# Gated linear attention with routed memories: the order of small and full-width products in the scan loop

## Chip, core and metric

One core of one Trainium2 chip. The metric is the device time of the whole program in microseconds, on that core. The engines are TensorE (PE: matmuls and transposes; its weight loads are PEld), VectorE (DVE), ScalarE (ACT), GpSimd (POOL, which issues the indirect DMAs) and SyncE (SP, which issues most of the others).

## What is computed

```python
x = x + attn(layernorm(x))      # x is (8, 512, 256)
x = x + moe(layernorm(x))       # 8 experts, top-k per expert

# attn: every token goes to 2 of 4 memories (at most 256 tokens each) and to a shared one
q, k, v = tx @ w_q, tx @ w_k[m], tx @ w_v[m]          # 4 heads, 32 and 64 wide
gk = log_sigmoid(tx @ w_gk1[m] @ w_gk2[m] + b_gk[m]) / 16
def step(S, (q, k, v, g)):      # over the tokens of a sequence
    S = S * exp(g)[..., None] + k[..., None] * v[..., None, :]
    return S, einsum('k,kv->v', q, S)
o = routed outputs, weighted and put back + shared output
o = o * rsqrt(mean(o * o) + eps) * norm_w * silu(x @ w_g)
return o @ w_o
```

All of it is float32.

## The kernel before

It has four parts. First the layer norm, the transposes of x and the gate product (0 to 60 us). Then the scan stage, 24 steps, which the change touches. Then the router's search for the tokens of each expert, and at last the experts. Every engine has its program written out by hand; engines meet at semaphores, and an engine that waits holds up everything behind it in its own program.

The scan stage treats a group of 512 tokens at a time: groups 0 to 6 and 23 are the shared memory's batches; groups 7 to 22 (`routed(g)`) are each two memories of one batch, half a group each. A group is cut into 8 chunks of 64 tokens. In the chunk, `scores` multiplies decayed keys `kd` and decayed queries `qd` (32 x 32 tiles of TensorE, 64 products, each two records in the trace); `masked` (L1028) copies them to `am` under the causal mask; `updates` (tiles of 64 x 32) multiplies keys and values of each chunk; `states` (L1047, L1049, L1053) chains the chunks on VectorE and writes `tst`; and `outputs` adds `qd` times `tst` and `am` times values. All four kinds are small products. The projections are full width: `gate` (512 or twice 256 columns), `keys`, `queries`, and `values` in two halves of 256 tokens. `keys_t` (L1577) and `rows_t` (L1570) are transposes. Nearly every product is issued by the helper at L1522, so the trace tells them apart by their tiles.

Decay factors come by a longer way. `gate` for group s+1 fills a bank, VectorE adds the bias (`gate_in`, L1016 or L1019), ScalarE makes a softplus of it in three steps (`softplus`, L692 to L696), VectorE finishes (`gate_log`, L1035), scans (`scan`, L1062) and takes distances (`distances`, L1071 to L1075), and ScalarE exponentiates (`decays`, L722 to L731). VectorE then multiplies keys and queries by them (`decayed_keys`, L1082; `decayed_queries`, L1089). ScalarE also empties banks: `values` (L685), `keys_in` (L714), `rows_in` (L679), and `group_out` (L704, L706), which takes the outputs of the group before and counts `d_ob`; TensorE waits for `d_ob` after `queries`.

In a step, TensorE's order is: values(s, 0), gate(s+1), outputs(s-1), keys(s), queries(s), the extra work, keys_t(s), values(s, 1), rows_t(s+2, 0), scores(s), rows_t(s+2, 1), updates(s). The extra work belongs to finished batches (`step_of(s, first)`: one batch every second step from `first` on): combine and head squares from step 11 (odd), `turned` and `gated` from 12 (even), `project` and `residual` from 13 (odd), `row_stats` from 14 (even), `norm_t` from 15 (odd), `route` and `router` from 16 (even). These products use the banks that `scores` writes, so `scores` waits for their readers.

GpSimd moves rows by indirect DMA, eight per slot: `scatter_slot` (L400) brings a batch's rows to its memories in steps 3 to 11, `gather_slot` (L407) brings outputs back in steps 10, 12 and so on to 22, and once behind the loop. SyncE loads the routed groups, stores the outputs (`store_group` waits for `d_ob`) and moves x. The choice of memories (`top`, `room`, `assign`, `counts`) runs in steps 0 to 2.

## Time and profile before

| what | value |
|---|---|
| median of 3 runs | 857.61 us (856.16 to 858.35) |
| profiled execution | 861.46 us, span 859.5 us |
| busy: TensorE, VectorE, ScalarE, GpSimd | 726.9, 392.4, 309.1, 237.3 us |
| chain that ended last | TensorE 80%, VectorE 10%, issue 5%, ScalarE 3% |
| scan stage, 60 to 489 us | TensorE idle about 29 us |

The span is the time from the first to the last instruction of the profiled execution. "Granted clock" is TensorE's clock as a share of 2.4 GHz; it is either 1.00 or 0.50, so a value between them says how long each level held. "issue" behind a gap says that the engine waited for nothing that the profile shows.

### The profile page before, as it was taken

Reading aid. Unit: us, or ns where it says so; the run is one execution under the profiler, and the core shown is the slowest. Engines: PE = TensorE matmul, PEld = TensorE weight load, DVE = VectorE, ACT = ScalarE, POOL = GpSimd, SP = SyncE. Lnnn points to the kernel's source line nnn. Section 1 sums busy time; section 2 is a strip of 40 time slices with the busy share of each in tenths; the row PEclk is TensorE's granted clock in tenths of the full one; section 3 lists DMA queues with packets and bytes.
Section 4 is the critical chain, followed back from the end, with each engine's and each line's share of the span. In section 5 each row is a group of like instructions: output and inputs, shape, how many; then the busy total and the mean of one; then the engine's idle time right before and its main releaser. Section 6 shows DMA issues by size and latency. Waiting matters only on the chain.

```text
span 859.5 us, 22577 instructions
## 1 busy us (share of the span) xinstructions
PE 726.9 (85%) x9727; PEld 552.5 (64%) x9727; DVE 392.4 (46%) x1132; ACT 309.1 (36%) x629; POOL 237.3 (28%) x232
## 2 busy tenths in 40 slices
PE   3998899989999999999999777202499999999994
PEld 3875665677777788888887556202347667766683
DVE  7517854544466666776576635698001001100111
ACT  2654433544354455565464324100141231123100
POOL 5300053554545031221213120000624342211222
PEclk9999988998899999999999966555599999999998
DMA  7940133333345244434254313700452454231212
GB/s 241 399 127 2 52 112 104 111 136 106 129 136 165 91 153 145 150 118 155 91 156 128 113 37 118 231 0 0 131 192 46 133 141 122 29 100 19 26 20 29
DMA packets 75435, 96.58 MB, mean 112 GB/s; under 512 B 11322, under 2 KB 67042, under 8 KB 74187
## 3 DMA queue, kind: packets, MB, share of 16 engines
q1 hardware_dynamic: 62506, 69.78, 24.8%
q0 software_dynamic: 12288, 25.12, 11.9%
q8 instruction: 76, 1.25, 0.6%
q10 hardware_dynamic: 544, 0.27, 0.1%
q14 instruction: 21, 0.16, 0.1%
HBM read 53.78 MB, written 41.55 MB: 111 GB/s over the span
## 4 chain that ended last, share of the span: by engine, by line
PE 80%; DVE 10%; issue 5%; ACT 3%; another core or an unknown queue 1%; DMA 1%; POOL 0%; DVEq 0%; POOLq 0%; ACTq 0%
PE bank L1522 49%; PE attn L1522 20%; PE bank L1480 3%; PE bank L1570 2%; DVE arena L1338 2%; PE bank L1577 1%; PE attn L1469 1%; PE attn L1835 1%; DVE gs L1402 1%; DVE gs L1397 1%; PE attn L1662 1%; DMA arena<-in_L_attn_x_dram 1%; PE attn L1686 1%; DVE st L909 0%
## 5 line engine op out<-in xcount | busy, mean ns | idle before, releaser
L1522 PE MATMUL bank<-xT,arena 128*128 128x256 f32 (+1 forms) x480 | 135.1, 429 | 0.7 <-ACT lg L641 0.7
L1522 PE MATMUL bank<-arena,xT 128*128 128x256 f32 (+1 forms) x448 | 133.2, 445 | 1.5 <-issue 1.5
L407 POOL DMA_INDIRECT big<-o_m,gidx x64 | 67.7, 1057 | 186.9 <-PE bank L1522 136.3
L1522 PE MATMUL attn<-arena 32*32 32x32 f32 (+3 forms) x5824 | 96.8, 221 | 22.0 <-issue 17.3
L1522 PEld LDWEIGHTS attn<-arena 32*32 32x32 f32 (+2 forms) x5824 | 79.8, 118 | 47.7 <-issue 37.6
L1522 PEld LDWEIGHTS bank<-xT,arena 128*128 128x128 f32 x480 | 90.2, 192 | 28.9 <-issue 17.4
L1522 PEld LDWEIGHTS bank<-arena,xT 128*128 128x128 f32 x448 | 88.8, 207 | 29.7 <-issue 17.8
L1449 DVE TENSOR_TENSOR arena<-bank,b2b 128x256 f32<-128x256 f32 x32 | 13.6, 425 | 203.3 <-PE bank L1522 203.3
L400 POOL DMA_INDIRECT x_c<-big,sidx x64 | 69.6, 1087 | 132.2 <-PE bank L1522 93.7
L479 POOL DMA_INDIRECT out_dram<-arena,idxs x32 | 49.7, 1553 | 131.2 <-DVE arena L1456 100.5
L466 POOL DMA_INDIRECT arena<-x_p,idxs x32 | 32.3, 1009 | 137.3 <-DVE idxs L1411 101.0
L1028 DVE COPY_PREDICATED arena<-causal,attn 128x1024 f32<-128x1024 int32 x24 | 31.6, 1316 | 79.1 <-PE attn L1522 79.1
L894 ACT ACTIVATE big<-attn,b1c 128x512 f32<-128x512 f32 x32 | 22.0, 687 | 116.7 <-PE attn L1522 116.7
L685 ACT ACTIVATE arena<-bank 128x512 f32<-128x512 f32 x48 | 28.7, 598 | 89.9 <-PE bank L1522 81.9
L1522 PE MATMUL bank<-xT,big 128*128 128x256 f32 x256 | 55.9, 379 | 0.0
L1522 PE MATMUL bank<-gs,big 128*128 128x256 f32 x256 | 55.7, 379 | 0.0
L1522 PEld LDWEIGHTS bank<-xT,big 128*128 128x128 f32 x256 | 48.6, 190 | 8.3 <-issue 1.9
L1522 PEld LDWEIGHTS bank<-gs,big 128*128 128x128 f32 x256 | 48.6, 190 | 7.9 <-issue 1.4
L886 ACT ACTIVATE arena<-attn 128x512 f32<-128x512 f32 x16 | 8.7, 594 | 73.9 <-PE attn L1835 71.8
L894 ACT ACTIVATE big<-bank,b1c 128x512 f32<-128x512 f32 x32 | 22.0, 688 | 32.9 <-PE bank L1522 32.9
L1049 DVE SCALAR_TENSOR_TENSOR arena<-arena,bank 128x64 f32<-128x64 f32 x112 | 31.5, 282 | 4.0
L1522 PE MATMUL attn<-arena,xT 128*128 128x512 f32 x64 | 30.6, 624 | 2.8 <-ACT arena L886 2.8
(240 smaller groups left out, 1063.7 us busy)
## 6 DMA issues: line engine op xcount, KB each, us to landing
x_c<-zeros SPq DMA_DIRECT2D x8, 1024.0 KB, 12.9
xT<-x_c SPq DMA_DIRECT2D x16, 512.0 KB
o_m<-arena SPq DMA_DIRECT2D x16, 512.0 KB
xT<-in_L_ffn_W_dram SPq DMA_DIRECT2D x8, 1024.0 KB, 8.6
gs<-in_L_ffn_W_dram SPq DMA_DIRECT2D x8, 1024.0 KB, 9.2
arena<-in_L_attn_x_dram SPq DMA_DIRECT2D x8, 512.0 KB, 7.7
xT<-in_L_attn_x_dram SPq DMA_DIRECT2D x8, 512.0 KB
out_dram<-xT SPq DMA_DIRECT2D x8, 512.0 KB, 5.3
```

The costliest lines, as they stand in the source:

```text
L400: nc.gpsimd.indirect_dma_start(x_c[b], bass.IndirectOffsetOnAxis(sidx[:, k, t:t + 1], 0), xn[:, t, :], None, bounds_check=MROWS - 1, oob_i ...
L407: nc.gpsimd.indirect_dma_start(og[:, b % 2, k, j, :], None, o_m[b], bass.IndirectOffsetOnAxis(gidx[:, k, t:t + 1], 0), bounds_check=MROWS ...
L466: nc.gpsimd.indirect_dma_start(xe[:, e % 3, j, :], None, x_p, bass.IndirectOffsetOnAxis(idxs[:, e, j:j + 1], 0), bounds_check=B * S - 1, o ...
L479: nc.gpsimd.indirect_dma_start(outf, bass.IndirectOffsetOnAxis(idxs[:, e, j:j + 1], 0), ye[:, e % 2, j, :], None, bounds_check=B * S - 1, ...
L685: nc.scalar.activation(vv[:, g % 2, 2 * h:2 * h + 2, :], bank[7].rearrange("p (j d) -> p j d", j=2), ACT.Copy).then_inc(d_vs, 1)
L894: nc.scalar.activation(ht[:, r, f, :], bank[2 + f % 4][:, :], ACT.Gelu_apprx_tanh, bias=b1c[:, col(f)]).then_inc(e_gl, 1)
L1028: nc.vector.copy_predicated(am[:, :, :, :], causal[:, :].bitcast(I32).unsqueeze(1).unsqueeze(1).to_broadcast([P, NH, TB, CH]), attn[:, :, ...
L1049: chained(nc.vector.scalar_tensor_tensor(vst[:, c, :], vst[:, c - 1, :], fe[:, g % 2, c - 1:c], u, ALU.mult, ALU.add))
L1338: ins = nc.vector.tensor_scalar(cmp[:, c, :], pt[:, :], cand[:, c:c + 1].bitcast(F32), None, ALU.is_ge, ALU.add, accum_out=reached[:, c:c ...
L1480: ins = nc.tensor.matmul(bank[4 + j][:, 0:D + M], xT[:, b, k, P * j:P * j + P], wgg[:, k, :], start=(k == 0), stop=(k == 1))
L1522: return nc.tensor.matmul(out_, l, r, start=a, stop=z, skip_group_check=True)
L1570: ins = nc.tensor.transpose(bank[4][:, P * j:P * j + P], xin[:, n % 2, j, P * k:P * k + P], ident[:, :])
```

## The change

TensorE's order becomes updates(s-1), gate(s+1), outputs(s-1), keys(s), queries(s), extra work, keys_t(s), scores(s, 0), values(s, 1), rows_t(s+2, 0), scores(s, 1), values(s+1, 0), rows_t(s+2, 1). The scores come in two parts of two token blocks (256 tokens) each, and `d_s` counts both. In `outputs` the product of `am` and values comes first and that with the states last. VectorE writes `kd` and `qd` (`qd` in two halves) ahead of the next scan, and `residual` follows the scan. In step 0 and 1 `top` is moved, in step 2 both `assign` stand behind the distances. The indirect DMAs wait for other events: behind `outputs`, behind each part of the scores, and behind `updates`. No arithmetic is added or removed, but for `qd`'s second instruction.

```diff
             def scatter_slot(b, s):
                 if b >= 2:
                     pool.wait_ge(scat[b % 2], 16 * 2 * TB * (b // 2))
-                pool.wait_ge(d_u, s)
+                pool.wait_ge(d_o, s)
                 scatter(b, 0, 3)
-                pool.wait_ge(d_o, s)
-                scatter(b, 3, 6)
-                pool.wait_ge(d_q, s + 1)
-                scatter(b, 6, 8)
+                pool.wait_ge(d_s, 2 * s + 1)
+                scatter(b, 3, 5)
+                pool.wait_ge(d_s, 2 * s + 2)
+                scatter(b, 5, 7)
+                pool.wait_ge(d_u, s + 1)
+                scatter(b, 7, 8)
 
             def gather_slot(b, s):
                 last = FIRST + 2 * b + 1
@@ -429,11 +431,11 @@
                 if b >= 2:
                     pool.wait_ge(f_oa, b - 1)
                 if b < LAST:
-                    pool.wait_ge(d_u, s)
-                    gather_back(b, 0, 3)
                     pool.wait_ge(d_o, s)
-                    gather_back(b, 3, 6)
-                    pool.wait_ge(d_q, s + 1)
+                    gather_back(b, 0, 4)
+                    pool.wait_ge(d_s, 2 * s + 1)
+                    gather_back(b, 4, 6)
+                    pool.wait_ge(d_s, 2 * s + 2)
                     gather_back(b, 6, 8)
...
@@ -825,9 +827,9 @@
 
             softplus(0)
             decays(0)
+            values(0, 0)
             for s in range(NG):
                 head, turn, route, stats = (step_of(s, f) for f in (11, 12, 15, 14))
-                values(s, 0)
                 if s + 1 < NG:
                     softplus(s + 1)
                 if 1 <= s <= NG:
@@ -849,6 +851,8 @@
                     decays(s + 1)
                 if routed(s + 2):
                     rows_in(s + 2, 1)
+                if s + 1 < NG:
+                    values(s + 1, 0)
...
             def decayed_queries(g):
@@ -1086,8 +1090,10 @@
                 dve.wait_ge(d_q, g + 1)
                 if g >= 1:
                     dve.wait_ge(d_o, g)
-                nc.vector.scalar_tensor_tensor(qd[:, :], bank[6], float(HDK) ** -0.5, eq[:, :],
-                                               ALU.mult, ALU.mult).then_inc(d_qd, 1)
+                for part in range(2):
+                    t = slice(CAP * part, CAP * part + CAP)
+                    nc.vector.scalar_tensor_tensor(qd[:, t], bank[6][:, t], float(HDK) ** -0.5, eq[:, t],
+                                                   ALU.mult, ALU.mult).then_inc(d_qd, 1)
...
             for s in range(NG):
                 head, turn, out_, stats, shift_, logit = (step_of(s, f) for f in (11, 12, 13, 14, 15, 16))
-                if s == 0:
-                    decayed_keys(0)
-                    decayed_queries(0)
                 if s >= 2:
                     states(s - 1)
+                if s == 1:
+                    states(0)
+                    top(0)
+                    decayed_keys(1)
                 if s + 1 < NG:
                     gate_in(s + 1)
-                if s == 0:
-                    top(0)
-                    masked(0)
-                    states(0)
-                if s == 1:
-                    decayed_keys(1)
-                    decayed_queries(1)
...
-                if s == 2:
-                    assign(0)
...
                 if shift_ is not None:
@@ -1249,29 +1246,33 @@
                     combine(head)
                 if turn is not None:
                     gated(turn)
+                if s + 1 < NG and s >= 2:
+                    gate_log(s + 1)
+                if s != 1:
+                    decayed_keys(s)
+                decayed_queries(s)
+                if s < 2:
+                    gate_log(s + 1)
                 if s + 1 < NG:
-                    gate_log(s + 1)
                     scan(s + 1)
-                if s >= 2:
-                    decayed_keys(s)
+                if out_ is not None:
+                    residual(out_)
                 if s + 1 < NG:
                     distances(s + 1)
-                if s >= 2:
-                    decayed_queries(s)
+                if s == 1:
+                    top(1)
+                if s == 2:
+                    assign(0)
+                    assign(1)
+                if logit is not None:
+                    router(logit)
+                if head is not None:
+                    head_squares(head)
+                if stats is not None:
+                    row_stats(stats)
+                masked(s)
                 if s == 1:
                     room()
-                if s == 2:
-                    assign(1)
-                if head is not None:
-                    head_squares(head)
-                if out_ is not None:
-                    residual(out_)
-                if logit is not None:
-                    router(logit)
-                if stats is not None:
-                    row_stats(stats)
-                if s >= 1:
-                    masked(s)
...
-            def scores(g):
-                pe.wait_ge(d_qd, g + 1)
-                if g >= 1:
...
-                for j, h, c, lo in product(range(TB), range(NH), range(2), range(2)):
+            def scores(g, part):
+                pe.wait_ge(d_qd, 2 * g + part + 1)
+                if part == 0:
+                    if g >= 1:
+                        pe.wait_ge(d_ob, g)
+                    turn, out_, route, logit = (step_of(g, f) for f in (12, 13, 15, 16))
+                    if turn is not None:
+                        pe.wait_ge(f_ont, 2 * turn + 2)
+                    if out_ is not None:
+                        pe.wait_ge(f_x1, 2 * out_ + 2)
+                    if route is not None:
+                        pe.wait_ge(f_xt2, 2 * route + 2)
+                    if logit is not None:
+                        pe.wait_ge(f_l8, logit + 1)
+                for j, h, c, lo in product((2 * part, 2 * part + 1), range(NH), range(2), range(2)):
...
             def outputs(g):
+                pe.wait_ge(d_am, g + 1)
+                for j in range(TB):
+                    for i in range(2):
+                        for c, h in ((0, i), (1, 3 - i), (1, 1 - i), (0, 2 + i)):
+                            s = slice(CH * c, CH * c + CH)
+                            mm(bank[h][half(c, h), HDV * j:HDV * j + HDV], am[s, h, j, :],
+                               vv[s, g % 2, j, HDV * h:HDV * h + HDV], j == 0, True)
                 pe.wait_ge(d_t, g + 1)
-                pe.wait_ge(d_am, g + 1)
                 heads = [lo // CH for _, lo, _ in pieces(g)]
-                opened = set()
                 for j in range(TB):
                     for c in range(2):
                         n = 2 * j + c
...
-                            mm(bank[h][half(c, h), HDV * j:HDV * j + HDV], qd[r, t], tst[r, n, :],
-                               (c, h) not in opened, False)
-                            opened.add((c, h))
-                for j in range(TB):
-                    for i in range(2):
-                        for c, h in ((0, i), (1, 3 - i), (1, 1 - i), (0, 2 + i)):
-                            s = slice(CH * c, CH * c + CH)
-                            ins = mm(bank[h][half(c, h), HDV * j:HDV * j + HDV], am[s, h, j, :],
-                                     vv[s, g % 2, j, HDV * h:HDV * h + HDV], False, True)
+                            ins = mm(bank[h][half(c, h), HDV * j:HDV * j + HDV], qd[r, t], tst[r, n, :], False, True)
                 ins.then_inc(d_o, 1)
...
             gate(0)
+            values(0, 0)
             for s in range(NG):
-                values(s, 0)
+                if s >= 1:
+                    updates(s - 1)
                 if s + 1 < NG:
                     gate(s + 1)
                 if s >= 1:
                     outputs(s - 1)
-                if s < NG:
-                    keys(s)
-                    queries(s)
+                keys(s)
+                queries(s)
                 if s >= 1:
                     pe.wait_ge(d_ob, min(s, NG))
                 if step_of(s, 12) is not None:
@@ -1754,17 +1754,19 @@
                     norm_t(step_of(s, 15))
                 if step_of(s, 16) is not None:
                     route(step_of(s, 16))
-                if s < NG:
-                    keys_t(s)
-                    values(s, 1)
-                    if s == 1:
-                        counts()
-                    if routed(s + 2):
-                        rows_t(s + 2, 0)
-                    scores(s)
-                    if routed(s + 2):
-                        rows_t(s + 2, 1)
-                    updates(s)
+                keys_t(s)
+                scores(s, 0)
+                values(s, 1)
+                if routed(s + 2):
+                    rows_t(s + 2, 0)
+                scores(s, 1)
+                if s + 1 < NG:
+                    values(s + 1, 0)
+                if s == 1:
+                    counts()
+                if routed(s + 2):
+                    rows_t(s + 2, 1)
+            updates(NG - 1)
             outputs(NG - 1)
             turned(LAST - 1, (4, 7))
             project(LAST - 1, 5)
```

## Rows read from the trace of the kernel before

**Rows 1.** The page: DMA queues, and the costliest groups (busy, mean ns, idle before).
```profile
q8 instruction: 76, 1.25, 0.6%
...
L400 POOL DMA_INDIRECT x_c<-big,sidx x64 | 69.6, 1087 | 132.2 <-PE bank L1522 93.7
```

**Rows 2.** Windows by stage: length, busy of each engine, granted clock, DMA share, GB/s.
```profile
104.00:148.40 44.40, 39.64 (x807) 26.58 (x797) 21.00 (x46) 15.05 (x31) 20.40 (x19) 0.85 0.32 105
...
196.00:235.00 39.00, 37.27 (x737) 30.39 (x730) 19.04 (x40) 16.00 (x31) 18.80 (x18) 0.87 0.36 122
...
284.00:289.00 5.00, 4.50 (x22) 3.62 (x23) 2.21 (x7) 0.53 (x1) 0.00 (x0) 0.66 0.35 104
```

**Rows 3.** Timeline of TensorE, step 4: start, duration, line, count, idle before.
```profile
139.16 0.33 PE L1522 MATMUL attn<-arena 32*32 32x32 f32 x5 [0.39 <-issue]
...
142.01 1.16 PE L1522 MATMUL bank<-arena 64*32 64x64 f32 x55 [0.96 <-issue]
143.10 3.78 PE L1522 MATMUL bank<-arena,xT 128*128 128x256 f32 x8
```

**Rows 4.** Timeline of TensorE, steps 13 and 14.
```profile
301.60 1.46 PE L1522 MATMUL attn<-arena 32*32 32x64 f32 x128
...
304.26 1.99 PE L1522 MATMUL bank<-arena,xT 128*128 128x256 f32 x8
306.09 1.89 PE L1522 MATMUL bank<-xT,arena 128*128 128x256 f32 x8
```

**Rows 5.** Waits of TensorE, 59.8 to 490 us (last row: 110 to 530): total, times, longest.
```profile
PE attn L1522 <- issue: 15.6, 33, 1.1
PE bank L1522 <- issue: 6.7, 7, 1.9
PE bank L1577 <- ACT arena L706: 1.9, 1, 1.9
...
PE attn L1522 <- DVE arena L1053: 4.0, 2, 2.9
```

**Rows 6.** Groups by form, TensorE, 59.8 to 490 us: busy, mean ns, idle before.
```profile
L1522 PE MATMUL attn<-arena 32*32 32x64 f32 x1536 | 40.6, 225 | 4.0 <-issue 3.7
L1522 PE MATMUL attn<-arena 32*32 32x32 f32 x1536 | 39.0, 200 | 7.4 <-issue 7.4
...
L1522 PE MATMUL bank<-arena 64*32 64x64 f32 x1191 | 20.5, 235 | 5.8 <-issue 5.2 <-ACT arena L685 0.6
```

**Rows 7.** Windows of 4 us; busy is PE, PEld, DVE, ACT, POOL.
```profile
104.00:108.00 4.00, 2.14 (x125) 1.79 (x115) 2.10 (x6) 1.18 (x4) 0.00 (x0) 0.93 0.01 4
...
192.00:196.00 4.00, 2.80 (x150) 2.01 (x152) 0.60 (x1) 1.97 (x7) 1.19 (x2) 1.00 0.21 73
...
300.00:304.00 4.00, 4.00 (x183) 3.37 (x185) 1.04 (x2) 2.79 (x8) 0.00 (x0) 1.00 0.02 4
```

**Rows 8.** Timeline of all engines, steps 4 and 5.
```profile
143.21 0.23 DVE L1047 COPY arena<-bank 128x64 f32<-128x64 f32 x1 [0.97 <-PE bank L1522]
...
145.37 0.63 DVE L1053 TENSOR_TENSOR arena<-arena 128x448 f32<-128x448 f32 x1
...
149.33 1.94 PE L1522 MATMUL attn<-arena 32*64 32x64 f32 x120
...
152.69 1.21 ACT L706 ACTIVATE arena<-attn 64x512 f32<-64x512 f32 x2
...
154.90 0.63 PE L1577 MATMUL bank<-ident,arena 128*128 128x128 f32 x4
```

**Rows 9.** Timeline of all engines, step 17.
```profile
370.38 1.27 DVE L1132 TENSOR_TENSOR xT<-attn,xT 128x512 f32<-128x512 f32 x2
...
371.37 1.08 ACT L769 ACTIVATE big<-attn 128x512 f32<-128x512 f32 x2 [2.28 <-PE attn L1686]
...
372.04 1.89 PE L1522 MATMUL bank<-arena,xT 128*128 128x256 f32 x8
...
373.77 0.60 PE L1570 MATMUL bank<-ident,xT 128*128 128x128 f32 x4
```

More of the change, by code:

```diff
@@ L728, in decays @@
                 if g >= 1:
-                    act.wait_ge(d_qd, g)
+                    act.wait_ge(d_qd, 2 * g)
                 for half_, at in ((lo, dec), (hi, cum)):
@@ L1024, in masked @@
             def masked(g):
-                dve.wait_ge(d_s, g + 1)
+                dve.wait_ge(d_s, 2 * g + 2)
                 if g >= 1:
@@ L1080, in decayed_keys @@
                 if g >= 1:
-                    dve.wait_ge(d_s, g)
+                    dve.wait_ge(d_s, 2 * g)
                 nc.vector.tensor_tensor(kd[:, :], bank[5], ek[:, :], ALU.mult).then_inc(d_kd, 1)
@@ L1226, in _ @@
                 head, turn, out_, stats, shift_, logit = (step_of(s, f) for f in (11, 12, 13, 14, 15, 16))
-                if s == 0:
-                    decayed_keys(0)
-                    decayed_queries(0)
                 if s >= 2:
                     states(s - 1)
+                if s == 1:
+                    states(0)
+                    top(0)
+                    decayed_keys(1)
                 if s + 1 < NG:
                     gate_in(s + 1)
-                if s == 0:
-                    top(0)
-                    masked(0)
-                    states(0)
-                if s == 1:
-                    decayed_keys(1)
-                    decayed_queries(1)
-                    top(1)
-                if s == 2:
-                    assign(0)
                 if s == FIRST:
@@ L1578, in keys_t @@
                 ins.then_inc(d_kp, 1)
-            def scores(g):
-                pe.wait_ge(d_qd, g + 1)
-                if g >= 1:
-                    pe.wait_ge(d_ob, g)
-                turn, out_, route, logit = (step_of(g, f) for f in (12, 13, 15, 16))
-                if turn is not None:
-                    pe.wait_ge(f_ont, 2 * turn + 2)
-                if out_ is not None:
-                    pe.wait_ge(f_x1, 2 * out_ + 2)
-                if route is not None:
-                    pe.wait_ge(f_xt2, 2 * route + 2)
-                if logit is not None:
-                    pe.wait_ge(f_l8, logit + 1)
-                for j, h, c, lo in product(range(TB), range(NH), range(2), range(2)):
+            def scores(g, part):
[13 more added lines that the diff above has]
+                for j, h, c, lo in product((2 * part, 2 * part + 1), range(NH), range(2), range(2)):
                     lo = lo * CH // 2
@@ L1603, in updates @@
                 pe.wait_ge(d_kt, g + 1)
-                pe.wait_ge(d_qd, g + 1)
+                pe.wait_ge(d_qd, 2 * g + 2)
                 pe.wait_ge(d_vs, 2 * g + 2)
```

## Prediction

> **What bounds the kernel now.** I read the page first. TensorE is by far the busiest engine and carries four fifths of the chain that ended last (the table above), so a change pays where TensorE idles or runs at its lower clock. The windows show where [rows 2]. The scan stage, 24 groups from 60 to 489 us, has two losses. The first is the granted clock: it is 0.85 in 104 to 148.4, 0.87 in 196 to 235 and 0.66 in 284 to 289; the stretch 417 to 422 reads the same as the last. A share of (1 - clock) of each stretch is lost: 0.15 x 44.4 = 6.7, 0.13 x 39 = 5.1, and 0.34 x 5 = 1.7 twice, 15.2 us in all. That is 30.4 us spent at 1.2 instead of 2.4 GHz. The price is seen on one row: the eight records of one `values` half take 3.78 us at the low level and 1.99 at the high one [rows 3, 4].
>
> The second loss is idle time of TensorE: 15.6 + 6.7 = 22.3 us in 40 gaps stand behind "issue", and only 5 us behind another engine [rows 5]. By form [rows 6] the gaps sit before small products: 3.7 + 7.4 = 11.1 us inside `scores`, 5.2 in `updates`, the other 6 in `outputs` and the start of `values`. The order explains the place. `scores` (128 records) and `updates` (48 or 56) stand together, with at most 4 transposes between, and in step 4 they show gaps, 0.39 us in the first and 0.96 in the second; right behind them the clock is at its low level [rows 3]. In step 13 the same sequence runs without a gap and the clock stays up [rows 4]. Windows of 4 us show both kinds of gap [rows 7]: with GpSimd issuing, TensorE is busy 2.80 of 4; without GpSimd and with DMA at 0.01 it is once busy only 2.14 of 4, where scores and updates follow each other; in a third it is busy all 4 with 183 products. So I take two causes: GpSimd's indirect DMAs against small products, and bursts of instructions longer than TensorE's supply.
>
> The program of TensorE comes in 76 packets, 1.25 MB, 16.4 KB each [rows 1]. The Trainium skill (Runtime: NRT & Kernel Launch, Instruction fetch mechanics) says an engine refills in 16 KiB blocks of 256 instructions and that crossing a block is mostly hidden. The packet size agrees; by the "hidden" part gaps would not follow bursts, and moving them would give nothing back (a rival below).
>
> **The change, part by part.** TensorE's work is the same; its order differs. Old step: values half 0, gate, outputs, keys, queries, extras, keys_t, values half 1, scores, updates. New: updates of the group before, gate, outputs, keys, queries, extras, keys_t, half the scores, values half 1, other half, next values half 0. No two kinds of small product touch any more: the longest run is 120 records, where it was 184.
>
> *Clock.* Low stretches follow a run of scores and updates with gaps. With 1.9 us of projection on both sides of every small burst I expect two of nine such stretches to stay (a stretch lasts 3.4 us by 30.4 / 9, 1.7 us lost each): 7 x 1.7 = -11.9. Bounds 0 and -15.2.
>
> *Gaps.* GpSimd issues eight indirect DMAs a slot, about 1.09 us each and a short pause [rows 1]. Before, three start at the end of `updates` and reach into `outputs`, and the last two run into `scores`. Now 3 or 4 start behind `outputs`, over keys and queries (3.7 us), two behind each half of the scores, over a values half (1.9 us). Of the 22.3 us I leave 5.0 in scores (half of each burst is still there), 1.0 in updates and 1.5 in outputs: -14.8. Bounds 0 and -20.8 (1.5 left).
>
> *More switches between small tiles and full ones.* A values half takes 1.83 us start to start behind updates (304.26 to 306.09) and 1.73 behind a transpose at full width (372.04 to 373.77) [rows 4, 9]: 0.10 for the way back. There is one more return per step: 23 x 0.10 = +2.3. Bounds 0, if the last small product is merely longer, and twice that, if the way there costs as much. The Trainium skill (TensorEngine Tiling (Array Packing), Key Properties) states that a change of tiling mode drains TensorE, which speaks against the change; the trace agrees with a small price, and the sum goes by the row.
>
> *New waits, plain steps.* Count from the end of updates(s-1). VectorE needs 2.8 us for `states` (143.21 to 146.00) [rows 8]. Old: that lay under values and gate, 3.7 us. New: gate is done at 1.85, the first half of `outputs` (scores times values, first now) at 2.8; the second half waits for the states to about 2.9. So 0.1 is lost in ungrouped steps, none in routed ones (six updates, 2.4 us). `gate_in` is behind the states, 1.05 us later than the gate's end. From gate end to the end of `group_out` it was 149.33 to 153.90, 4.57 us, and keys_t began at 154.90, behind the queries [rows 8]: slack 1.0, now used up. About +0.2 in five steps, +1.0. Keys_t finds `kd` ready: keys end 1.85 us before queries and the product of 0.67 now goes before the scan. The split costs VectorE about 0.15 us a step (a 256-column operation is about 0.42), behind its own waits for scores.
>
> *New waits, steps with extra work.* The first half of the scores now comes 1.73 + 0.53 = 2.27 us earlier, and that was the cover of everything `scores` waits for. In step 17 keys_t ends at 372.04; the two copies of `norm_t` end at 372.45, `residual` at 371.65 [rows 9]. So +0.4 in the five steps with `norm_t`, +0.4 in step 13 (project's last half plus a residual half of 0.64 less keys_t), +0.3 in steps 12 and 14 (copy of the turned tile 0.75, less 0.43): +3.2. From step 16 on the router's add (0.19) ends inside keys_t.
>
> *First steps.* Step 1: `gate_in(2)` is behind states, top and keys, so group_out and the 1.9 us wait on it [rows 5] grow by 0.9. Step 2: gate(3) waits for `room`, behind masked and counts: +0.5. Both `assign` (20 operations, 4.5 us) now stand ahead of masked(2), which holds back states(2) by 1.3. Sum +2.7. Step 23 has no gate: the wait for states was 4.0 - 2.9 = 1.1 [rows 5], now about 1.5: +0.4. SyncE's queue: the load of a routed group waits for all eight scatters, which now end about 1.3 us into the next step, and it is used a step later; the store of a group stands behind it but waits for `d_ob` 8 us into the step anyhow. The last two gathers end 0.4 us into the next step and `combine` starts 4 us in; a landing of 2 us fits, with 1.5 to spare.
>
> *Behind the loop.* TensorE waits 2.9 us for states(23) [rows 5]; half of `outputs`, 1.0 us, now runs there: -1.0.
>
> Sum: -11.9 - 14.8 + 2.3 + (1.0 + 3.2 + 2.7) + 0.4 - 1.0 = -18.1 us. It is made against the profiled execution (861.46; span 859.5), which lies 3.85 above the median of the runs, 857.61; I take the same difference there: **839.5**. The chip tells 0.3% (2.6 us) from no change.
>
> **Rivals.**
> 1. *More comes back.* All low stretches go and 1.5 us of gaps stay: -15.2 - 20.8 + 8.6 = -27.4, 830; with the new waits at half, 827. For it: step 13 shows the old sequence gapless. Against: gaps appear also without GpSimd.
> 2. *Half comes back.* Gaps move into the halves and four or five low stretches remain: -7.6 - 7.4 + 8.6 = -6.4, 851. For it: the old gaps of 0.4 us come after 39 to 46 small products, and a half has 64.
> 3. *It changes nothing that can be told.* A third comes back, 12 us at most, less 8.6, and up to 2.3 more for the switches: 855 to 860.
> 4. *Slower, nothing comes back.* Gaps and clock belong to the number of small instructions and to GpSimd: +8.6, 866. Against it: the gaps differ by step and place with the same count of instructions. The section of the Trainium skill on instruction fetch, named above, speaks for it, since hidden fetches would leave the length of a burst without effect.
> 5. *Slower, first half of scores late.* It loses its cover of 2.27 us. If whatever it waits for (the residual, `ont`, `d_ob`) arrives just in time for the old place, the loss is 2.27 x 12 = 27 us in place of 3.2, so 863. It decides from 1.5 us in each of the twelve steps with extra work. Against it: in step 17 the last of these is 0.4 us late, not 2.27 [rows 9].
>
> **How the numbers follow.** Forecast (833 to 848) 0.47, rival 1 0.14, rival 2 0.17, rival 3 0.09, rival 4 0.07, rival 5 0.06. Faster is 0.47 + 0.14 + 0.17 = 0.78, same 0.09, slower 0.13. The range leaves out the slower cases and the lowest end of rival 1: 826 to 858.
>
> **What would show it.** The granted clock in 104 to 240 us near 1.00 (clock step), else rival 2 or 4. TensorE's waits: "issue" near 7 to 8 us in place of 22.3, with few behind `updates`; GpSimd's DMAs under full-width products. New waits behind VectorE's states or ScalarE's copies before the first scores half, near 0.4 us each: if they are above 1.5, rival 5. The scan stage, 429 us long, should last about 412. The search and the experts behind it should not change. I would be wrong most easily in how many gaps remain, for no row shows split scores.

## The result and the profile after

The changed kernel takes 869.75 us (median of 4 runs, 867.53 to 871.63), the kernel before beside it 857.98 (856.16 to 861.04): the ratio is 1.0138, 95% interval 1.0105 to 1.0171. It is slower by 1.4%, where 839.5 was forecast. Its profiled execution took 871.63 us, its span is 869.9; the span of before was 859.5. Of all runs below one, at 864.08 us, lay over 1.5% above the fastest of its kernel, and that kernel's ratio ("before, paced 2") leaves it out.

The page of the changed kernel, the rows that answer to [rows 1], with TensorE's share of the span:

```profile
PE 738.2 (85%) x9727; PEld 553.0 (64%) x9727; DVE 394.9 (45%) x1156; ACT 306.4 (35%) x629; POOL 235.0 (27%) x232
...
q8 instruction: 76, 1.25, 0.6%
...
L407 POOL DMA_INDIRECT big<-o_m,gidx x64 | 70.5, 1101 | 185.9 <-PE attn L1523 148.5
...
L400 POOL DMA_INDIRECT x_c<-big,sidx x64 | 64.5, 1008 | 146.2 <-PE attn L1523 123.7
```

The work is the same. What grew is the scan stage. I measure it as "the loop" below, from the start of `keys_t` in step 0 to its start in step 23, read from TensorE's timeline: 69.0 to 485.1 before, 69.5 to 496.7 after, 416.1 us against 427.2. Ahead of it 0.4 us were lost, behind it 1.2 gained. The windows, to set beside [rows 2]:

```profile
104.00:148.40 44.40, 39.48 (x879) 24.88 (x877) 26.55 (x69) 16.31 (x33) 16.02 (x16) 1.00 0.32 105
...
196.00:235.00 39.00, 36.15 (x802) 29.30 (x804) 18.88 (x42) 16.30 (x32) 17.80 (x19) 1.00 0.39 132
284.00:289.00 5.00, 4.50 (x30) 3.53 (x30) 1.30 (x1) 0.19 (x1) 2.31 (x3) 0.66 0.22 69
```

The granted clock is 1.00 where it was 0.85 and 0.87, as forecast. Over the whole loop it is less good: six stretches of 3.4 us at 1.2 GHz, 20.5 us, where nine made 30.7. TensorE's waits from 59.8 to 500 us, to set beside [rows 5]:

```profile
PE attn L1523 <- issue: 12.5, 34, 0.5
PE bank L1523 <- issue: 6.3, 15, 0.6
PE bank L1578 <- ACT arena L708: 3.6, 1, 3.6
PE attn L1523 <- DVE arena L1057: 2.9, 2, 1.5
PE attn L1523 <- ACT big L771: 2.0, 5, 0.4
```

"issue" is 18.8 us in 49 gaps and not 7 to 8. The longest is 0.6 us; before it was 1.9. So the gaps changed in kind: of those behind "issue" from 59 to 500 us the kernel before has eight over 0.8 us, 10.7 us in all, and this one none; the shorter ones rose from 14.8 us to 18.8. A gather step shows where the short ones are. TensorE from 358 us:

```profile
358.63 0.82 PE L1523 MATMUL attn<-arena 32*32 32x64 f32 x64 [0.28 <-issue]
359.37 1.99 PE L1523 MATMUL bank<-arena,xT 128*128 128x256 f32 x8
361.20 0.60 PE L1571 MATMUL bank<-ident,xT 128*128 128x128 f32 x4
361.73 0.79 PE L1523 MATMUL attn<-arena 32*32 32x64 f32 x41
362.98 0.47 PE L1523 MATMUL attn<-arena 32*32 32x64 f32 x23 [0.46 <-issue]
363.38 1.99 PE L1523 MATMUL bank<-arena,xT 128*128 128x256 f32 x8
365.21 0.60 PE L1571 MATMUL bank<-ident,xT 128*128 128x128 f32 x4
365.74 0.84 PE L1523 MATMUL bank<-arena 64*32 64x64 f32 x44
367.02 0.32 PE L1523 MATMUL bank<-arena 64*32 64x64 f32 x4 [0.44 <-issue]
```

and GpSimd's timeline in the same stretch:

```profile
357.08 1.01 POOL L407 DMA_INDIRECT big<-o_m,gidx  x1 [0.30 <-issue]
360.23 1.00 POOL L407 DMA_INDIRECT big<-o_m,gidx  x1 [2.14 <-PE attn L1523]
361.54 1.00 POOL L407 DMA_INDIRECT big<-o_m,gidx  x1 [0.30 <-issue]
364.23 1.00 POOL L407 DMA_INDIRECT big<-o_m,gidx  x1 [1.70 <-PE attn L1523]
365.54 1.00 POOL L407 DMA_INDIRECT big<-o_m,gidx  x1 [0.30 <-issue]
```

Read the two together. The full-width products at 363.38 (eight records) run at their usual speed with a DMA beside them. (Counts of small products here and below are counts of records, two to a product.) A burst of small products runs for about 41 records and stops until 0.4 to 0.5 us behind the end of GpSimd's record: 362.54 and 362.98, 366.54 and 367.02. The pair of DMAs released by one half of the scores starts 0.9 us later, its first lies under the values half, and its second under the next small burst. In steps 3 to 22 it is so in all steps with DMAs but those where the products between ran at 1.2 GHz and gave it time (steps 10, 12, 18 and 22). A stalled burst costs more than its recorded gap: scores part 1 took 363.38 - 361.73 = 1.65 us with a gap of 0.46, where the same burst without a DMA takes 0.77 (382.98 to 383.75, step 17). The lost 0.88 us are nearly twice the gap. In all, this kernel's scores and updates run 31 us over their clean lengths at the full clock. 13 of its updates are stalled under a DMA (1.1 to 1.9 us in place of 0.76, 9.8 us lost); in the kernel before, none was. The Trainium skill (Perfetto Trace Analysis, Tensor Engine Instruction) says that the end of a TensorE record is estimated from the instruction's size, so a gap between records need not be all of a stall; the trace agrees.

By groups of steps the loop changed in three ways (scatter steps 3 to 9; then even steps 10 to 22, which gather, and odd ones 11 to 21):

| us | first 3 | 7 scatter | 7 gather | 6 odd | loop |
|---|---|---|---|---|---|
| before | 49.3 | 124.2 | 134.7 | 107.9 | 416.1 |
| changed | 50.3 | 119.7 | 152.6 | 104.6 | 427.2 |
| before, no indirect DMAs | 49.2 | 107.3 | 130.2 | 100.6 | 387.2 |
| changed, no indirect DMAs | 50.3 | 105.2 | 132.5 | 102.4 | 390.4 |

### The profile page after: what moved, and what is told of

Its sections match the earlier page's. It is cut to its first block, busy times and chain, and to the rows that moved or that the text cites. A ratio compares the mean times of both kernels' runs of the same rounds, so it can differ in the third digit from the quotient of the medians.

```text
span 869.9 us, 22576 instructions
## 1 busy us (share of the span) xinstructions
PE 738.2 (85%) x9727; PEld 553.0 (64%) x9727; DVE 394.9 (45%) x1156; ACT 306.4 (35%) x629; POOL 235.0 (27%) x232
## 3 DMA queue, kind: packets, MB, share of 16 engines
q0 software_dynamic: 12288, 25.12, 11.9%
## 4 chain that ended last, share of the span: by engine, by line
PE 79%; DVE 10%; issue 6%; ACT 3%; DMA 1%; POOL 0%; another core or an unknown queue 0%; DVEq 0%; POOLq 0%; ACTq 0%
PE bank L1523 49%; PE attn L1523 21%; PE bank L1481 4%; DVE arena L1339 2%; PE bank L1571 2%; PE attn L1837 1%; PE attn L1470 1%; DVE gs L1398 1%; ACT big L771 1%; DVE gs L1403 1%; PE bank L1578 1%; PE attn L1661 1%; DMA arena<-in_L_attn_x_dram 1%; DVE st L913 0%; DVE big L924 0%
## 5 line engine op out<-in xcount | busy, mean ns | idle before, releaser
L1523 PE MATMUL bank<-xT,arena 128*128 128x256 f32 (+1 forms) x480 | 137.9, 435 | 1.0 <-ACT lg L643 0.8
L1523 PE MATMUL bank<-arena,xT 128*128 128x256 f32 (+1 forms) x448 | 131.0, 437 | 0.7 <-issue 0.6
L1523 PE MATMUL attn<-arena 32*32 32x64 f32 (+3 forms) x5824 | 100.8, 221 | 23.6 <-issue 15.9
L407 POOL DMA_INDIRECT big<-o_m,gidx x64 | 70.5, 1101 | 185.9 <-PE attn L1523 148.5
L1523 PEld LDWEIGHTS bank<-xT,arena 128*128 128x128 f32 x480 | 87.9, 191 | 30.3 <-issue 18.1
L1450 DVE TENSOR_TENSOR arena<-bank,b2b 128x256 f32<-128x256 f32 x32 | 13.6, 425 | 203.8 <-PE bank L1523 203.8
L400 POOL DMA_INDIRECT x_c<-big,sidx x64 | 64.5, 1008 | 146.2 <-PE attn L1523 123.7
L1523 PEld LDWEIGHTS bank<-arena,xT 128*128 128x128 f32 x448 | 85.0, 198 | 29.5 <-issue 17.4
L694 ACT ACTIVATE arena<-arena 128x512 f32<-128x512 f32 x24 | 15.2, 632 | 78.2 <-DVE arena L1023 47.5
```

The lines of the kernel that those rows point to most:

```text
L400: nc.gpsimd.indirect_dma_start(x_c[b], bass.IndirectOffsetOnAxis(sidx[:, k, t:t + 1], 0), xn[:, t, :], None, bounds_check=MROWS - 1, oob_i ...
L407: nc.gpsimd.indirect_dma_start(og[:, b % 2, k, j, :], None, o_m[b], bass.IndirectOffsetOnAxis(gidx[:, k, t:t + 1], 0), bounds_check=MROWS ...
L1523: return nc.tensor.matmul(out_, l, r, start=a, stop=z, skip_group_check=True)
```

## The experiments

Theory: the order moves GpSimd's indirect DMAs under small products more often than it moves them away, and splitting the scores has a price of its own. Rival: the price is in the order alone (more returns, later operands); another: the DMAs cost by their traffic, wherever they stand. Twelve kernels ran, in three groups with runs of the kernel before beside each (medians 861.8, 858.7 and 863.3 us), so ratios and loops are compared and not times across groups. A loop is that of one trace: the changed kernel's two differ by 2.2 us. "DMAs" is the loop less that of the same order without indirect DMAs, and so holds what the clock lost with them too.

| kernel | ratio, interval | loop | DMAs |
|---|---|---|---|
| before | 1 | 416.1 | 28.9 |
| changed | 1.0138, 1.0105 to 1.0171 | 427.2 | 36.8 |
| changed, again | 1.0141, 1.008 to 1.0202 | 425.0 | 34.6 |
| changed, the old events for GpSimd | 1.0779, 1.0699 to 1.0859 | 487.6 | 97.2 |
| changed, scores together | 1.012, 1.0033 to 1.0207 | 428.1 | 51.7 |
| before, paced | 0.9971, 0.9942 to 0.9999 | 414.3 | 27.1 |
| before, paced 2 | 0.9894, 0.9852 to 0.9937 | 407.4 | 20.2 |
| changed, paced | 1.041, 1.035 to 1.0469 | 454.7 | 64.3 |
| together, paced | 0.9977, 0.9948 to 1.0006 | 416.3 | 39.9 |
| together, paced 2 | 0.9949, 0.9931 to 0.9968 | 416.9 | 40.5 |
| before, no DMAs | 0.9541, 0.9469 to 0.9614 | 387.2 | |
| changed, no DMAs | 0.953, 0.946 to 0.960 | 390.4 | |
| changed, no DMAs, late split | 0.95, 0.9482 to 0.9518 | 382.6 | |
| changed, no DMAs, scores together | 0.9486, 0.943 to 0.9542 | 376.4 | |

**1 and 2. Both orders without the scan stage's 128 indirect DMAs.** `scatter` and `gather_back` return at once, and the waits for them go:

```diff
 def scatter(b, lo, hi):
-    for j, k in moves[lo:hi]:
-        nc.gpsimd.indirect_dma_start(...)
+    return
```

> The kernel before without its 128 indirect DMAs of the scan stage (scatter and gather_back return at once, their waits are gone), so the memories read zeros and nothing is put back: this part of the computation is left out. Theory 1 (the new order itself is dear): about 845 to 850 us; most of the 22.3 us of gaps are bursts of instructions and stay. Theory 2 (the indirect DMAs stall small products): gaps in scores and outputs vanish, only those in updates stay, 835 to 842 us.

> The changed kernel with the same part left out. Theory 1: it stays slower than the same kernel before by 8 to 15 us, because each step pays about 0.6 us for one more entry into small products and for a first scores half that waits for its queries. Theory 2: the loss is gone or reversed, within 3 us of the kernel before in the same form, because no stall is left that could fall into a small burst.

824.62 us (821.73 to 827.0) and 824.18 (821.19 to 827.22). The twelve microseconds between the kernels are gone, as the second theory had it for the changed kernel; for the kernel before, both theories had expected at least 10 us more. The loops differ by 3.2 us (387.2 and 390.4), the medians by 0.4, so the parts of the order and of the DMAs in the loss are known to some 3 us only. TensorE's waits in 59.8 to 490 us, before without DMAs:

```profile
PE bank L1506 <- issue: 11.9, 10, 2.0
...
PE attn L1506 <- issue: 1.8, 4, 0.8
```

and the changed kernel without them:

```profile
PE bank L1507 <- issue: 2.5, 2, 1.3
```

So the long gaps aren't GpSimd's: they stand in the old order without it, and the new order leaves two of them, 2.5 us. The short ones are: none is left in the changed order. That the new order still gains nothing means it has a price at least as large as what it gains by these gaps.

**3. The changed kernel with the old events for GpSimd** (3 behind the updates, 3 behind the outputs, 2 behind the queries):

```diff
-pool.wait_ge(d_o, s)
+pool.wait_ge(d_u, s)
 scatter(b, 0, 3)
...
+pool.wait_ge(d_q, s + 1)
+scatter(b, 6, 8)
```

> The changed kernel with the indirect DMAs behind the events of before (updates, outputs, queries: 3, 3 and 2). Theory 1: 868 to 871 us, no change. Theory 2: 860 to 866 us, since the last DMA of a pair no longer ends inside the second half of the scores and inside updates.

931.36 us (929.33 to 933.91), 60 us above both theories. The same eight DMAs of a step cost 60 us more of the loop than with the changed kernel's events. In one step scores part 0 takes 4.2 us in place of 0.77. TensorE:

```profile
209.66 0.64 PE L1521 MATMUL attn<-arena 32*32 32x64 f32 x38
210.47 0.31 PE L1521 MATMUL attn<-arena 32*32 32x32 f32 x4 [0.17 <-issue]
211.21 0.32 PE L1521 MATMUL attn<-arena 32*32 32x32 f32 x4 [0.43 <-issue]
211.96 0.32 PE L1521 MATMUL attn<-arena 32*32 32x32 f32 x5 [0.43 <-issue]
212.72 0.30 PE L1521 MATMUL attn<-arena 32*32 32x32 f32 x5 [0.44 <-issue]
213.46 0.46 PE L1521 MATMUL attn<-arena 32*32 32x64 f32 x8 [0.44 <-issue]
```

and GpSimd:

```profile
210.05 1.81 POOL L400 DMA_INDIRECT x_c<-big,sidx  x1 [0.30 <-issue]
212.16 0.98 POOL L400 DMA_INDIRECT x_c<-big,sidx  x1 [0.30 <-issue]
```

After 38 records four or five come every 0.75 us until GpSimd is done. The clock pays as well: 78 us of this loop are at 1.2 GHz, 58 more than with the changed kernel's events, so 29 of the 60 us are the clock's.

**4 and 5. Scores together,** with and without DMAs (the last leaves the 128 indirect DMAs out):

```diff
-scores(s, 0)
 values(s, 1)
 ...
+scores(s, 0)
 scores(s, 1)
```

> The changed kernel, but TensorE issues both halves of the scores back to back behind values half 1 (and rows_t), so there is one entry less and qd is long ready. Theory 1: 14 us less than the changed kernel, 855 to 858 us. Theory 2 alone: one stalled burst less in about 20 steps at 0.8 us, against gaps that come back inside a longer burst: 862 to 868 us.

> The changed kernel without indirect DMAs (that part of the computation is left out) and with both halves of the scores back to back behind values half 1. It prices the split by itself against after_no_idma: clean steps there take 15.04 us against 14.73 in the order before. If the split and its wait for the queries cost 0.3 us in plain and 0.5 in heavy steps: 7 to 10 us less, unless gaps in the longer burst come back (about 10 us in before_no_idma), which would leave it equal, 820 to 826 us.

874.07 us (869.33 to 878.91) with DMAs, above both theories, and 813.68 (809.51 to 815.26) without. Splitting changes little beside the DMAs and costs 14.0 us of loop without them (390.4 less 376.4; the two were timed in different groups, their ratios differ by 0.4% only and the intervals overlap, so the size is that of two traces). Together, the four DMAs that the scores release go off one behind the other and reach the updates, 14 of which are stalled, hence much of the 51.7 us of DMA cost (13.6 of it is the clock). Here full-width products stall as well: in eight steps `gate`, right behind such updates and with the DMA still at work, has a gap of 0.16 to 0.52 us before or among its first five records.

**6. Split, but later** (no DMAs): part 0 behind the values half, part 1 behind the next one.

```diff
-scores(s, 0)
 values(s, 1)
 ...
-scores(s, 1)
+scores(s, 0)
 values(s + 1, 0)
+scores(s, 1)
```

> The changed kernel without the 128 indirect DMAs of the scan stage (left out: scattered and gathered rows are not moved), and with part 0 of the scores behind the second half of the values, part 1 behind the next step's first half: still two parts with full products between them, but part 0 no longer stands right behind the transposed keys, where it waits for VectorE's decayed queries. Without DMAs the changed order took 824.2 and with the parts back to back 813.7. Theory A (the 10.5 us are that wait, about 0.3 us in each of 23 steps = 7, and the split itself 0.15 us a step = 3.5): about 817, range 815 to 820. Theory B (they are the price of coming back to small products once more): no change, 822 to 826. A new wait of the outputs for the masked scores, which have 1.9 us less cover here, would add up to 1 us a step.

819.84 us (818.88 to 821.75), inside theory A's range. A plain step reads it exactly; the changed order without DMAs:

```profile
180.84 0.60 PE L1562 MATMUL bank<-ident,arena 128*128 128x128 f32 x4
181.58 0.84 PE L1507 MATMUL attn<-arena 32*32 32x64 f32 x64
182.35 1.99 PE L1507 MATMUL bank<-arena,xT 128*128 128x256 f32 x8
184.18 0.60 PE L1555 MATMUL bank<-ident,xT 128*128 128x128 f32 x4
184.71 0.84 PE L1507 MATMUL attn<-arena 32*32 32x64 f32 x64
```

and with the later split:

```profile
179.98 0.60 PE L1562 MATMUL bank<-ident,arena 128*128 128x128 f32 x4
180.41 1.89 PE L1507 MATMUL bank<-arena,xT 128*128 128x256 f32 x8
```

The four transposes take 0.74 us in front of scores part 0 and 0.43 in front of values: 0.3 us is a wait for `qd`, whose first part VectorE can only write when the queries are done, and TensorE's waits do not list it, since the transposes' modelled records cover it. VectorE's row in the changed order fits: the two halves of `qd` are written from 181.10 on, the first is done halfway, and the scores start at 181.58.

```profile
181.10 0.76 DVE L1081 SCALAR_TENSOR_TENSOR arena<-bank,arena 128x256 f32<-128x256 f32 x2 [0.80 <-issue]
```

A plain step (8) is 15.04 us in the changed order, 14.78 with the later split and 14.49 together: 0.26 for that wait, 0.29 for two parts in place of one.

**7. The changed kernel once more,** as it is.

> The changed kernel once more, as the reference of this set: 1.2 to 1.6% slower than the kernel before, by every theory.

869.2 us (867.31 to 872.81), span of the profile 865.6: the result stands, and 10.2 us at 1.2 GHz in place of 20.5 show how much of the clock term is chance (5 us).

**8 to 12. Where the DMAs go off.** Only the events that GpSimd waits for change. Behind updates (U), outputs (O), scores (S, or S0 and S1):

| kernel | scatter steps | gather steps |
|---|---|---|
| before | U3 O3 queries 2 | U3 O3 queries 2 |
| changed | O3 S0 2 S1 2 U1 | O4 S0 2 S1 2 |
| before, paced | S1 U3 O4 | U2 O6 |
| before, paced 2 | S2 U2 O4 | U2 O4 S2 |
| changed, paced | U2 O4 S0 1 S1 1 | O6 S0 1 S1 1 |
| together, paced | U1 O5 S2 | O5 S2 U1 |
| together, paced 2 | U1 O4 S3 | O4 S3 U1 |

The scatter of "before, paced 2":

```diff
-pool.wait_ge(d_u, s)
-scatter(b, 0, 3)
-pool.wait_ge(d_o, s)
-scatter(b, 3, 6)
-pool.wait_ge(d_q, s + 1)
-scatter(b, 6, 8)
+pool.wait_ge(d_s, s)
+scatter(b, 0, 2)
+pool.wait_ge(d_u, s)
+scatter(b, 2, 4)
+pool.wait_ge(d_o, s)
+scatter(b, 4, 8)
```

> The kernel before with other events for its indirect DMAs: scatter 1 behind scores, 3 behind updates, 4 behind outputs; gather 2 behind updates, 6 behind outputs, so that most of them run under full-width products. Theory 2 (while GpSimd handles an indirect DMA, TensorE gets few instructions: small products starve and full-width ones don't notice): 12 to 18 us less than before, about 1.2 us in each of 7 scatter steps and 6 gather steps. Rival theory 3 (it is the traffic of these DMAs that delays TensorE's instruction fetches, whatever runs meanwhile): the same bytes, so within 3 us of before.

> The changed kernel with other events: scatter 2 behind updates, 4 behind outputs, 1 behind each half of the scores; gather 6 behind outputs and 1 behind each half. Theory 2: the stalls in the second half of the scores and in updates go, a smaller one comes back in the first half: 12 to 20 us less than the changed kernel, at or below the kernel before. Theory 3: within 3 us of the changed kernel.

> The changed kernel with both parts of the scores back to back and GpSimd's eight indirect DMAs of a step let go behind other stages: scatter one behind the updates, five behind the outputs, two behind the scores; gather five behind the outputs, two behind the scores, one behind the next updates. Nothing is left out. Theory 1 (what costs is an indirect DMA that falls under small products; five DMAs need 5 to 6 us and keys with queries last 3.6, so some of it remains): most of the 45 to 60 us that the DMAs cost in this order goes down to some 30, so 813.7 + 30 = about 844, range 836 to 852, faster than both kernels. Theory 2 (the DMAs cost by their traffic or count, wherever they stand): the same as with the scores together before, about 870.

> The same with one DMA moved from behind the outputs to behind the scores: scatter 1, 4, 3; gather 4 behind the outputs, 3 behind the scores, 1 behind the next updates. Nothing is left out. Theory 1: the fifth DMA behind the outputs no longer reaches the small products behind keys and queries, but the third behind the scores (3 x 1.0 us after 0.9 us, so until 4 us behind them) falls into the updates, which start 2.5 us behind the scores: 0 to 6 us slower than the version with 1, 5, 2. Theory 2: no difference.

> The kernel before with its indirect DMAs let go elsewhere: scatter two behind the scores, two behind the updates, four behind the outputs; gather two behind the updates, four behind the outputs, two behind the scores. Nothing is left out. The earlier try had six behind the outputs in the gather steps, which reached the small products behind the queries and gave back there the 5 us that the scatter steps had gained. Theory 1: about 849 to 854, 5 to 9 us faster than before. Theory 2: no difference from before, 858.

Medians: before, paced 856.04 us (852.22 to 862.03); changed, paced 894.01 (892.38 to 898.3); together, paced 863.04 (856.78 to 867.34) and 858.75 (857.95 to 862.55); before, paced 2 856.49 (849.05 to 864.08). "Traffic only" is refuted by "changed, paced" and by the third experiment: in one order the same 128 DMAs cost 34.6 to 97.2 us. My sizes were mostly off. "Before, paced" was to gain 12 to 18 us and gained 0.3%, by itself what the traffic theory says. "Changed, paced" was a bad plan: one DMA behind each half of the scores leaves both later bursts clean, but the fourth behind the outputs reaches scores part 0 (2.56 us) and those behind the updates the outputs (2.80 in place of 1.80), at six the gather steps take 22 to 26 us. "Together, paced" stayed 13 us above what I expected (0.9977 of 858.7 is 857, and 844 was said). "Together, paced 2" was to be 0 to 6 us slower than it and was not. The step 7 of "together, paced" shows why it lost, TensorE:

```profile
190.53 0.67 PE L1521 MATMUL attn<-arena 32*32 32x64 f32 x39
191.69 0.32 PE L1521 MATMUL attn<-arena 32*32 32x32 f32 x4 [0.49 <-issue]
192.44 1.08 PE L1521 MATMUL attn<-arena 32*32 32x32 f32 x85 [0.44 <-issue]
193.45 2.00 PE L1521 MATMUL bank<-arena,xT 128*128 128x256 f32 x8
195.28 0.60 PE L1569 MATMUL bank<-ident,xT 128*128 128x128 f32 x4
195.81 0.76 PE L1521 MATMUL bank<-arena 64*32 64x64 f32 x43
197.03 0.35 PE L1521 MATMUL bank<-arena 64*32 64x64 f32 x5 [0.46 <-issue]
```

GpSimd:

```profile
191.07 0.97 POOL L400 DMA_INDIRECT x_c<-big,sidx  x1 [0.30 <-issue]
194.32 0.97 POOL L400 DMA_INDIRECT x_c<-big,sidx  x1 [2.28 <-PE attn L1521]
195.59 0.97 POOL L400 DMA_INDIRECT x_c<-big,sidx  x1 [0.30 <-issue]
```

Scores need 193.45 - 190.53 = 2.92 us where 1.39 is clean, updates 1.50 where 0.76 is: 2.27 us, and the step is 16.76 us against 14.49 without DMAs, the same 2.27. From the end of the outputs to the scores are 6.3 us (184.27 to 190.53), and five DMAs need 0.9 + 5 x 1.3 = 7.4: four of them cost nothing, the fifth does. "Before, paced 2" is faster than both kernels, by 1.1% against before: its scatter steps take 116.4 us (124.2 before), its gather and odd steps together 242.0 (242.6). But its loop has 13.7 us at 1.2 GHz where before's has 30.7, which is 8.5 of the 8.7 us between them: what stalls it spared directly and what the clock gave, by them or by chance, one trace can't part.

## Why the prediction was wrong

The loop lost 11.1 us. Idle time rose by 2.0 (26.5 to 28.5), the clock gave back 5.1 (half of 30.7 less 20.5), and 14.3 are neither: periods less idle time less half of the low stretches went from 374.2 to 388.5 us. (In the idle time "issue" fell by 3.5 and the waits for other engines rose by 5.5.) Without DMAs that last figure goes from 364.8 to 374.6, so 9.8 are the order's own and 4.5 the part of stalls that no gap records. By the steps of the prediction:

- *Gaps, -14.8: failed, and it is the step that turned the sign.* "Two behind each half of the scores, over a values half (1.9 us)" left out that a pair starts 0.9 us late and lasts 2.3, so it ends 3.2 us behind its event, in the next small burst. The recorded gaps fell by 3.5 us (22.3 to 18.8), and each stall costs nearly twice its gap. The loop lost 36.8 us to DMAs in place of 28.9: +7.9 where the step had counted on a gain. Had the 14.8 come back, the loop would have been shorter than before's. The other half of the step was right: gaps that stand without any GpSimd (12.0 us of the loop) fell to 2.5 when no two small bursts touched. The Trainium skill (Runtime: NRT & Kernel Launch, Instruction fetch mechanics) calls the crossing of an instruction block mostly hidden; if these gaps are such crossings, which no run shows, they were not hidden in the old order.
- *Switches, +2.3: right in kind, a third of the size.* The split costs 0.29 us in a plain step against 0.10 for a return, and 6.9 over the loop (periods less idle time and low clock, 371.5 with the later split and 364.6 together). The Trainium skill (TensorEngine Tiling (Array Packing), Key Properties) says that every change of tiling mode drains TensorE. The trace agrees with a price of that kind; how much of it is the drain was not measured.
- *New waits in plain steps, +1.0: missed.* The first half of the scores waits 0.26 us for `qd` in a plain step, 3.1 us over the loop that no wait lists (374.6 less 371.5). The prediction checked `kd` there and not `qd`. With the switches that is 10.0 us where 3.3 were counted, nearly what the order gains without DMAs: 9.6 us of "issue" (12.05 to 2.48 over the loop) and 1.7 of clock (half of 10.2 less 6.8). The waits for other engines below make the rest of the 3.2 us that the loop is longer there.
- *Waits in steps with extra work, +3.2: right.* The copies of `norm_t` hold TensorE 2.0 us in five steps, 0.39 each in step 17 (from [rows 9] 0.4 was read), two others 0.4 each.
- *Clock, -11.9: less than half.* It rose where it was said to, but six stretches were low where two were counted: at 248 and 285 us right behind scores with two or three stalls, at 398 and 477 in or behind a scores half with a gap of 0.28 and 0.22 us before it (the same gap at 358 us had no such effect), at 87 behind the 3.6 us wait of step 1 and at 487 behind a 1.4 us wait for the states. -5.1 (-10.2 in the second profile).
- *First steps, +2.7: about right.* The wait in step 1 grew by 1.7 us (0.9 was said), and the states of group 2 hold TensorE 1.5 us in step 3 (1.3 was said). The time up to step 3 grew by 1.4 us only, since a gap of 1.9 us left it. *Step 23, +0.4:* +0.3. *Behind the loop, -1.0:* -1.2.

Rival 4 came nearest in time, 866, but not by its reason: the gaps did not stay with the count of instructions. Its remark "to GpSimd" was the half that held. Rival 2's remark, that gaps come after 39 to 46 small products and a half has 64, was the fact to work out: with it, and GpSimd's start 0.9 us behind its event, most stalls could have been placed from before's own trace.

What stays open: what a stall under a DMA is made of (the profile shows only that TensorE waits for nothing it lists; that instructions come too slowly is read from their steady four or five at a time), what the long gaps are made of (a packet of the instruction queue lies near each, but one lies near any point), and how the six low stretches are picked, since two profiles of one kernel differ. The gain of "together" without DMAs (813.7 us) was not reached with them; fewer or longer indirect DMAs were not tried.

## What to carry to other kernels

Before reordering TensorE, lay GpSimd's indirect DMAs over the new order, each from its real start (event + 0.9 us, then 1.3 us apiece), and see which bursts of small products they meet; nearly all of the direct cost was there. Keep them under full-width products, and expect a burst of more than 40 records of small products under one to lose 1.7 to 1.9 times the gap that the trace shows (0.76 us for 0.44 in the updates, 0.88 for 0.46 in the scores). A split burst wants its operands early: put it behind other work, not right behind the stage that makes its last input.

## What was not expected of the hardware

While GpSimd is at an indirect DMA, TensorE behaves as if starved of instructions: after 38 to 46 records of small products it gets four or five every 0.75 us until some 0.4 us behind GpSimd's record. That costs 0.7 to 0.9 us in a burst of 48 to 64 records and 3.4 in one that meets more DMAs. Full-width products show no loss unless they follow a stalled burst with the DMA still at work (the eight `gate` gaps above): a values half takes 1.83 us start to start with a DMA beside it (359.37 to 361.20) and without (380.62 to 382.45, step 17). An estimate from these rows: eight full-width records in 1.83 us are 3.3 in 0.75 us, fewer than the four or five that still come. The same 128 DMAs cost 34.6 to 97.2 us of the loop in the changed order and 20.2 to 28.9 in the old one, by nothing but their start, the clock's part included.
